# Self attention of the last layer: the value products of a block of keys in one visit of four products of 512 queries, in place of two visits of 256

## The reference

```python
def _L3_ffn_ref(x, ln1_g, ln1_b, ln2_g, ln2_b, wq, bq, wk, bk, wv, bv, wo, bo, ...):
    hn = _layernorm(x, ln1_g, ln1_b)
    q = (hn @ wq + bq).reshape(b, s, NH, D).transpose(0, 2, 1, 3)
    k = (hn @ wk + bk).reshape(b, s, NH, D).transpose(0, 2, 1, 3)
    v = (hn @ wv + bv).reshape(b, s, NH, D).transpose(0, 2, 1, 3)
    scores = jnp.einsum('bhqd,bhkd->bhqk', q, k) / jnp.sqrt(jnp.float32(D))
    attn = jax.nn.softmax(scores, axis=-1)
    o = jnp.einsum('bhqk,bhkd->bhqd', attn, v)
    x = x + (o.transpose(0, 2, 1, 3).reshape(b, s, h) @ wo + bo)
    ...
```

## Time and profile before

| | |
|---|---|
| median of 3 runs | 1114.28 us (1109.92, 1114.28, 1120.05) |
| profiled execution, first to last instruction | 1110.5 us |
| its mean granted TensorE clock | 0.889 of full speed |
| TensorE (PE) busy | 905.3 us, 82% of the span |
| VectorE (DVE) busy | 607.6 us, 55% |
| ScalarE (ACT) busy | 437.0 us, 39% |
| the self attention stage | about 740 to 1010 us of the span |
| steps of the maximum in it (L2022) | 128, from 740.4 to 997.4 us |

### The profile page before, as it was taken

One profiled execution on the slowest core, in us unless ns is written; L12 is line 12 of the kernel. 1 busy time (PEld: TensorE's weight loads), 2 busy tenths in 40 slices (PEclk: granted clock), 3 DMA queues, 4 the chain that ended last, 5 costly groups with the idle time before them and its releaser, 6 DMA issues.

```text
span 1110.5 us, 15394 instructions
## 1 busy us (share of the span) xinstructions
PE 905.3 (82%) x5738; PEld 492.8 (44%) x5738; DVE 607.6 (55%) x1629; ACT 437.0 (39%) x750; POOL 225.0 (20%) x226
## 2 busy tenths in 40 slices
PE   4788866987768786496898899868889889887988
PEld 2334544654424443375465334323334334344766
DVE  4455664445554534343733454557777777773644
ACT  2344323332333222110331333335767667665333
POOL 1100050434161211234321100100000000200354
PEclk9799897998977867598789799987999999999899
DMA  9900011232137000311001000000000000102030
GB/s 284 304 23 1 1 35 47 70 95 63 45 111 231 26 22 30 89 35 49 19 1 45 1 2 1 1 1 1 1 1 1 2 1 2 40 1 73 29 106 15
DMA packets 43248, 52.87 MB, mean 48 GB/s; under 512 B 6078, under 2 KB 32830, under 8 KB 42488
## 3 DMA queue, kind: packets, MB, share of 16 engines
q1 hardware_dynamic: 37864, 42.61, 12.6%
q0 software_dynamic: 5312, 9.29, 2.6%
HBM read 37.45 MB, written 23.26 MB: 55 GB/s over the span
## 4 chain that ended last, share of the span: by engine, by line
PE 58%; DVE 19%; issue 9%; ACT 5%; DMA 4%; POOL 4%; SPq 1%; POOLq 0%; DVEq 0%; ACTq 0%
PE PS L182 50%; DVE KB L2022 5%; DVE KB L1624 2%; PE PS L659 2%; POOL RB L2323 1%; DVE Ht L1538 1%; POOL d L2313 1%; PE PS L1136 1%; DVE st L1525 1%; DVE ON L1691 1%; DMA RB<-d 1%; ACT KB L1432 1%; POOL dbuf L2243 1%; POOL ve L2216 1%; DVE OT L1666 1%
## 5 line engine op out<-in xcount | busy, mean ns | idle before, releaser
L2022 DVE TENSOR_REDUCE KB<-PS 128x2 fp32r<-128x1024 f32 x128 | 154.5, 1221 | 47.3 <-PE PS L182 46.2
L1286 ACT ACTIVATE PT<-PS 77x512 f32<-77x512 f32 x192 | 98.1, 590 | 169.8 <-PE PS L182 169.8
L182 PE MATMUL PS<-CX 32*77 32x512 f32 (+2 forms) x896 | 125.5, 570 | 18.1 <-DVE OT L1666 6.8
L2216 POOL TENSOR_TENSOR ve<-ve,nh 128x4 f32<-128x4 f32 x40 | 41.7, 1042 | 446.0 <-DVE ve L1533 445.8
L1624 DVE TENSOR_REDUCE KB<-PS 128x16 fp32r<-128x1232 f32 x48 | 69.1, 1440 | 75.0 <-PE PS L182 75.0
L182 PE MATMUL PS<-RA,RB 128*128 x152 | 85.3, 645 | 8.7 <-issue 3.9
L1452 ACT ACTIVATE PT<-PS 128x1024 f32<-128x1024 f32 x74 | 75.6, 1023 | 35.6 <-PE PS L182 34.6
L182 PE MATMUL PS<-QB,KB 64*128 64x512 f32 x256 | 59.1, 459 | 20.9 <-DVE KB L2022 18.5
L182 PEld LDWEIGHTS PS<-CX 32*128 32x128 f32 (+1 forms) x896 | 48.6, 191 | 61.9 <-issue 16.6
L182 PE MATMUL PS<-KB,QB 64*128 64x512 f32 x256 | 65.7, 514 | 5.3 <-DVE KB L2022 3.2
L182 PE MATMUL PS<-PT,VB 77*32 77x512 f32 x384 | 56.6, 664 | 8.0 <-DVE KB L1624 6.3
(11 more groups left out here) (318 smaller groups left out, 1626.7 us busy)
## 6 DMA issues: line engine op xcount, KB each, us to landing
d<-d SPq DMA_DIRECT2D x2, 1472.0 KB, 10.0
dbuf<-in_c_fill SPq DMA_DIRECT2D x1, 2580.0 KB, 20.2
RB<-d SPq DMA_DIRECT2D x10, 256.0 KB, 3.1
o<-CX SPq DMA_DIRECT2D x10, 256.0 KB, 2.5
RA<-in_l_w SPq DMA_DIRECT2D x1, 2304.0 KB, 10.3
RB<-d SPq DMA_DIRECT2D x4, 514.0 KB, 4.4
d<-OT SPq DMA_DIRECT2D x2, 1024.0 KB, 6.7
RB<-in_l_w SPq DMA_DIRECT2D x1, 2048.0 KB, 11.1
```

The costliest lines, as they stand in the source:

```text
L182: return e.matmul(o, l, r, start=first, stop=last, skip_group_check=True)
L1286: e.activation(slot[s][0:NK, :], PS[0:NK, 4 + j, :], ACT.Exp, bias=0.0, scale=a.scale).then_inc(*expd(i, r, j))
L2022: e.tensor_reduce(o, PS[:, k:k + 2, :], AX, ALU.max).then_inc(*rmax("s", s, t, p2))
L2216: e.tensor_tensor(ve[:, 8 * par + 4:8 * par + 8], ve[:, 8 * par:8 * par + 4], nh[:, :], ALU.pow).then_inc(*rstd(*key))
```

## The change

`fourth` no longer walks over the two halves of the queries. A visit is now four products of 512 queries, one for each head, and there is one for each block of keys instead of two. The step count of `fourth` drops from nine to five, on TensorE as on ScalarE and VectorE (`idle(4)` for `idle(8)`, `idle(5)` for `idle(9)`). In the table of `order` the visit of block 0 stands at 0.8 (before: halves at 0.675 and 0.8), block 1 at 0.05 of the next iteration (0.925 and 0.05), block 2 at 0.3 (0.175 and 0.3), block 3 at 0.485 (0.425 and 0.485).

```diff
                 for c in range(4):
                     w.wait_ge(*expd.at("s", s, c, 1))
-                    for q in (0, 256):
-                        for j in range(4):
-                            E = exps[eslots.of(weighed, "s", s, c, j % 2)]
-                            m = mm(e, PS[32 * j:32 * j + 32, 7, q:q + 256], vv[:, c, 4 * g + j, :],
-                                   E[:, 512 * (j // 2) + q:512 * (j // 2) + q + 256], c + q == 0, c == 3)
-                        if q:
-                            m.then_inc(*weighed("s", s, c))
-                            for p2 in range(2):
-                                weighed.also("s", s, c, p2)
-                        yield
+                    for j in range(4):
+                        E = exps[eslots.of(weighed, "s", s, c, j % 2)]
+                        m = mm(e, PS[32 * j:32 * j + 32, 7, :], vv[:, c, 4 * g + j, :],
+                               E[:, 512 * (j // 2):512 * (j // 2) + 512], c == 0, c == 3)
+                    m.then_inc(*weighed("s", s, c))
+                    for p2 in range(2):
+                        weighed.also("s", s, c, p2)
+                    yield
                 yield
...
-                    streams.append((islice(values[i], 3), [0.675, 0.8, 0.925]))
+                    streams.append((islice(values[i], 1), [0.8]))
...
-                    streams.append((values[i - 1], [0.05, 0.175, 0.3, 0.425, 0.485, 0.505]))
+                    streams.append((values[i - 1], [0.05, 0.3, 0.485, 0.505]))
```

More of the change, by code:

```diff
@@ L1457, in fourth @@
                 b, g = s // 4, s % 4
-                yield from idle(8)
+                yield from idle(4)
                 w.wait_ge(*weighed.at("s", s, 3))
@@ L2031, in fourth @@
             def fourth(s):
-                yield from idle(9)
+                yield from idle(5)
             def tail4(b):
```

## The result

The changed kernel takes **1129.45 us** (median of 4 runs, 1126.31 to 1138.48) against 1112.25 us of the kernel before in the runs beside it. The ratio is **1.0155, 95% interval 1.0107 to 1.0204**: slower by 17 us. The forecast was 1116 us with a range of 1101 to 1133; the time lies inside the range, but not where the likeliest case put it (1104 to 1125), and the range held only because it reached up to a rival's full price.

A forecast was written before the change was run, and what follows sets the result against it. The prediction took PE as the bound in self attention, with PE and DVE waiting for each other in turn. From 1114.3 us it took 0.4 for the iterations and added 2 for the clock: 1116 us, range 1101 to 1133.

The forecast's parts named there:

- the likeliest case: Whole kernel: the forecast's own case, a time between 1104 and 1125 us, chance 0.54.
- The bound: Self attention: PE and DVE wait in turn; a T starts no earlier than 1.82 us after the previous slot's S.
- The price of a visit of 512: Value products on PE: a doubled visit takes 1.00 us, ends 0.95 and 1.06, against 0.57 for each half.
- visits get no cheaper: Rival on the value products: a doubled visit takes 1.14 us, 9 us more than in the sum: 1125 us; chance 0.04.
- The borders: Slots 1, 5 and 7: T followed by S at once saves 0.10 us, 48 times: 4.8 us, up to 9.
- The walk through the iterations: Four iterations, one of each kind, 873.7 to 941.1 us: -0.7 + 0.3 + 0.2 + 0.1 = -0.1 us; -0.4 for sixteen.
- the bare slots' 4.6 us: Two slots with one doubled visit and nothing else: 0.29 us more for each block, 18.6 us at all 64.
- Idle before T: Stage after the change: idle ended by DVE's maximum (L2022) up from 21 to about 30 us; DVE's idle about as before.
- The clock: Stage's granted clock: two more stretches at 1.2 GHz allowed for, 2 us; below 0.93 the forecast is wrong.
- The clock falls more often: Rival: a stretch at 1.2 GHz in each iteration instead of one in four, 14 us more: 1128 us; chance 0.08.
- The stalls win: Rival: in slots 1, 5, 7 the second T waits for the maximum, 0.29 us a block: 1133 us; chance 0.19.
- PE's work counts in full: Rival: other work fills the stalls everywhere, so PE's saved work counts, 18 us less: 1096 us; chance 0.15.

The follow-up runs named there:

- the whole visit of block 3: Kernel before with only block 3, whose two halves both stood in slot 3, as one visit of 512; no slot emptied: ratio 0.9969.
- the repeat: The changed kernel as it is, run again in a third set on another chip against the kernel before: 1127.85 us, ratio 1.0133.
- even slots: Changed kernel with its four visits of 512 moved to slots 5, 7, 1 and 3, every second slot: ratio 1.0165 to the kernel before.
- the fills: Changed kernel with T of slots 1, 4, 5, 7 issued three times (ratio 1.0081), twice (1.0056), or three times in units 9 to 15 only (1.008).

## Why the prediction was right, and where it was wrong

- **The bound** (PE and DVE wait for each other through three bank pairs, a T no earlier than 1.82 us after the S of the slot before): right. It stands in the changed kernel to the hundredth (888.32 to 890.13, 1.81), and moving one visit into the one slot that lacked it halved the idle before T and won 6 us.
- **The price of a visit of 512**, 1.00 us with 0.95 and 1.06 as ends: right, measured at 1.00 twice. The case that visits get no cheaper did not come.
- **The borders**, 0.10 us each: right (896.63 to 896.87; the whole visit of block 3, ratio 0.9969).
- **The walk through the iterations**, -0.1 us for four: wrong by 1.4. At the same clock four became 1.3 us longer (67.80 to 69.13). The iteration with projections became 0.45 us shorter where 0.7 was said; the other three, said to become 0.1 to 0.3 longer, became 0.5 to 0.75 longer. Why the walk was short there is not shown. Over sixteen iterations that is about 5 us in place of -0.4. It lies between the walk and the bare slots' 4.6 us for four (sixteen blocks of 0.29), nearer the walk. Ten iterations together became 3.5 us longer; one more stretch at the lower clock (about 1.5 us, 19.1 for 17.6) is among them.
- **Idle before T**, 21 to about 30 us: right, 20.9 to 29.7. That DVE's idle before its maxima would stay about as before was not: 44.0 us became 55.1.
- **The clock**: this is the step that failed most. "I allow for two more such stretches in the stage", 2 us, was mis-sized. Over 756 to 1003 us the granted clock fell from 0.96 to 0.89; in time at 1.2 GHz (twice the share missing from 1) that is 20 and 54 us of 247, so 34 us more, where two stretches had been allowed for. They came mostly in a row, in the last iterations, and there the stage lost 12.8 us. By the estimate above the clock's part of the loss is 9 to 12 us where 2 were in the sum. The test that the prediction itself gave, a clock below 0.93, came out: by its own sign the forecast was wrong.
- **The rivals.** *The clock falls more often*, priced at 1128 and given a chance of 0.08, is the case that came, 1129.45, though not as it was drawn: not once in each iteration, and with part of the loss from the order. That the number fits so well is luck. The experiments bear out its mechanism: added PE work in the idle brought the clock to 0.98 and won 7 us; work left out of the emptied slots took it down and lost 5. *The stalls win* named the right place and 1133 us, but of its price of 0.29 us a block only 0.08 was seen (1.3 us over sixteen blocks). *PE's work counts in full* fell: 9 us of it were worth 5 to 7 in slot 3, and 27 us in slots 1, 5 and 7 nothing.
- **The chances.** Slower by over 1% had 0.29. That the time lies in the stated range is owed to the width of the range, which went up to the stalls' full price, and not to the sum, whose two terms for the order and the clock were both too small. The stalls and the clock had been treated as two cases; the idle that the forecast itself expected (9 us more before T) was enough to bring the clock down.

Left open: why the clock stays low for so long at times, while the records show PE busy (17.9 of 19.0 us from 934 to 953), and what sets the place, which the repeat had elsewhere; and why even slots cost more at the same clock. That emptied slots bring the clock down and work put into them brings it back is shown by the fills, early, late and within one execution, and by the work left out. Whether it is the length of single gaps or the idle in all that counts is not shown: the table has one number for each trace.

## What to carry to other kernels

Before merging two pieces of work of the busiest engine, look at what each of them covers: a piece that stands between a product and the wait for its bank is cover, and its removal frees nothing; one that stands beside another piece is worth most of its time (5 to 7 of 9 us here). Where TensorE and VectorE pass bank pairs to each other, see that every slot has its piece of filler before making the filler smaller. And count idle on TensorE for more than itself: here 14 us more of it (25.0 to 38.8) went with a clock of 0.90 for 0.98, also over work that never waited.

## What the runs showed of the hardware that was not expected

- Adding 27 us of repeated products to TensorE made a kernel of 1129 us 7 us faster, through a granted clock of 0.98 for 0.89 in the stage. Taking 27 us of products away from the kernel before made it 0.4% slower, at a mean clock of the whole program of 0.862 for 0.880.
- Stretches at 1.2 GHz are not always short: behind the slow start of the stage they cost the kernel before 1.4 us now and then, in the changed one the clock was 0.68 and 0.57 over 19.0 and 23.4 us, in a part where the records show TensorE busy for 94% and 81% of the time.
- Each change between S or T (64 x 128 weights) and a visit (128 x 32) costs about 0.10 us, while a second visit right behind the first adds 0.43 us in place of 0.57: 1.00 us for two halves together, 1.14 apart. By the Trainium skill, "TensorEngine Tiling (Array Packing)", Key Properties, a change of the tiling mode drains TensorE; the trace agrees in that each change costs time, and does not show what takes it.
